# One more mask of every sixteen on GpSimd in a fused pre-norm graph attention block

## The reference

```
h = maximum(layernorm(x), 0)
q, k, v = h @ Wq + bq, h @ Wk + bk, h @ Wv + bv       # split into 16 heads
scores = q @ k.T / sqrt(32);  scores = -inf where adj == 0
out = x + (softmax(scores) @ v) @ Wo + bo
```

## Time and profile before

| what | value |
|---|---|
| median of 3 runs | 1587.12 us (1585.24 to 1588.4) |
| the profiled execution | 1589.11 us, span 1587.3 us |
| mean granted TensorE clock | 0.985 of full speed |
| busy share of PE, DVE, ACT, POOL | 97%, 91%, 89%, 47% |
| masks on GpSimd, on VectorE | 438, 586 |

### The profile page before, as it was taken

One profiled execution on the slowest core, in us unless ns is written; L12 is line 12 of the kernel. 1 busy time (PEld: TensorE's weight loads), 2 busy tenths in 40 slices (PEclk: granted clock), 3 DMA queues, 4 the chain that ended last, 5 costly groups with the idle time before them and its releaser, 6 DMA issues.

```text
span 1587.3 us, 27500 instructions
## 1 busy us (share of the span) xinstructions
PE 1547.2 (97%) x7489; PEld 1040.7 (66%) x7489; DVE 1442.1 (91%) x3505; ACT 1418.9 (89%) x3433; POOL 752.6 (47%) x674
## 2 busy tenths in 40 slices
PE   7899999999999999999999999999999999999987
PEld 6566666666666666666666666676676666666644
DVE  7889899999999989999998999999899999998976
ACT  4899898998989899898998989999899999989884
POOL 3244455454454554455354354454445455353442
PEclk9899999999999999999999999999999999999988
DMA  7544444434444344444434444344444534444320
GB/s 230 124 110 104 129 111 108 137 95 139 101 129 119 101 139 103 130 111 114 132 97 131 101 131 117 93 144 105 125 113 103 143 93 139 101 114 111 99 73 27
DMA packets 154064, 183.63 MB, mean 116 GB/s; under 512 B 67748, under 2 KB 69808, under 8 KB 153904
## 3 DMA queue, kind: packets, MB, share of 16 engines
q1 hardware_dynamic: 149024, 179.76, 42.2%
q10 hardware_dynamic: 4888, 2.11, 0.6%
HBM read 54.79 MB, written 16.78 MB: 45 GB/s over the span
## 4 chain that ended last, share of the span: by engine, by line
PE 56%; DVE 16%; ACT 12%; SPq 7%; issue 7%; DMA 1%; ACTq 1%; DVEq 0%; POOL 0%
PE psP L858 24%; PE psO L950 10%; PE ps L920 10%; PE ps L932 9%; ACT ps L530 6%; DVE ps L688 6%; SPq L283 4%; ACT probs L586 4%; DVE probs L702 3%; SPq L324 2%; DVE neg_max L688 1%; DVE oT_lo L722 1%; ACTq L492 1%; DVE stats L613 1%; DVE probs L705 1%
## 5 line engine op out<-in xcount | busy, mean ns | idle before, releaser
L444 POOL TENSOR_TENSOR probs<-probs,keep_k 128x512 int32<-128x512 int32 x438 | 573.5, 1333 | 559.1 <-ACT probs L586 558.7
L688 DVE CUSTOM_DVE_ANT_0 ps<-ps,bias_q 128x512 f32<-128x512 f32 x1024 | 704.1, 694 | 100.4 <-PE ps L920 94.1
L530 ACT ACTIVATE ps<-ps,neg_max 128x512 f32<-128x512 f32 x1024 | 691.7, 675 | 66.4 <-DVE neg_max L688 49.0
L586 ACT ACTIVATE probs<-ps 128x512 f32<-128x512 f32 x1024 | 622.6, 609 | 52.4 <-PE psO L950 28.0
L920 PE MATMUL ps<-k_stack,q_stack 96*128 96x512 f32 x1024 | 431.5, 422 | 18.7 <-ACT ps L530 13.5
L932 PE MATMUL ps<-q_stack,k_stack 98*128 98x512 f32 x1024 | 421.1, 412 | 5.3 <-ACT probs L586 4.1
L702 DVE SCALAR_TENSOR_TENSOR probs<-turned,probs 128x512 f32<-128x512 bf16 x512 | 371.3, 726 | 5.4 <-ACT probs L586 4.5
L920 PEld LDWEIGHTS ps<-k_stack,q_stack 96*128 96x128 f32 x1024 | 194.8, 190 | 133.6 <-ACT ps L530 53.7
L950 PE MATMUL psO<-probs,v_sb 128*32 128x512 f32 x2048 | 251.7, 609 | 1.2 <-issue 1.2
L932 PEld LDWEIGHTS ps<-q_stack,k_stack 98*128 98x128 f32 x1024 | 196.9, 192 | 72.9 <-ACT probs L586 41.4
L530 ACT ACTIVATION_READ_ACCUMULATOR ps<-ps,neg_max 128x1 f32 x1024 | 223.0, 218 | 0.0
(11 more groups left out here) (87 smaller groups left out, 1891.9 us busy)
## 6 DMA issues: line engine op xcount, KB each, us to landing
k_stack<-oT_hi SPq DMA_DIRECT2D x380, 64.0 KB, 2.0
q_stack<-y_tile SPq DMA_DIRECT2D x360, 64.0 KB, 2.0
x_tile<-in_x_dram SPq DMA_DIRECT2D x66, 256.0 KB, 3.1
y_tile<-in_x_dram SPq DMA_DIRECT2D x62, 256.0 KB, 2.9
out_dram<-y_tile SPq DMA_DIRECT2D x62, 256.0 KB, 2.0
turned<-in_adj_dram SPq DMA_DIRECT2D x61, 256.0 KB, 3.0
q_stack<-part_hi SPq DMA_DIRECT2D x240, 64.0 KB, 2.0
k_stack<-oT_lo SPq DMA_DIRECT2D x196, 64.0 KB, 2.0
```

Source lines behind the costliest of these rows:

```text
L444: nc.gpsimd.tensor_tensor(bits, bits, keep_k[:, kt // 2, :], ALU.mult).then_inc(gpsimd_masked, 1)
L530: nc.scalar.activation(item, item, ACT.Exp, scale=-1.0, bias=neg_max[:, g % 2, col:col + 1], accum_out=exp_sum[:, col:col + 1]).then_inc(e ...
L586: nc.scalar.activation(probs[:, (SLOTS * b + n) % P_RING, :], ps2[:, n % 2, :], ACT.Exp, scale=SCALE).then_inc(exp2_done, 1)
L688: nc.vector.tensor_tensor_reduce(bank1(k, ("s", u)), bank1(k, ("s", u)), bias_q[:, qt, :], -SCALE, 3.0e38, ALU.add, ALU.min, neg_max[:, g ...
```

## The change

Tile 7 of every group joins the list of GpSimd, so that GpSimd masks key tiles 1 and 3 whole (tiles 4 to 7 and 12 to 15) and VectorE key tiles 0 and 2. It holds for all groups but the last two of the last batch. The waits by count follow from the same list.

```
-ON_GPSIMD, LAST_ON_GPSIMD = (4, 5, 6, 12, 13, 14, 15), (4, 12)
+ON_GPSIMD, LAST_ON_GPSIMD = (4, 5, 6, 7, 12, 13, 14, 15), (4, 12)
```

## The result

The kernel with tile 7 on GpSimd has a median of 1588.97 us over 20 runs (1587.03 to 1592.57), beside 1585.33 us (1581.75 to 1588.61) for 20 runs of the kernel before on the same chip. The ratio is 1.0027, with a 95% interval of 1.002 to 1.0035: slower by some 4 us (the medians differ by 3.6 us, and the ratio makes 4.3 us of them), where +3.7 us was forecast.

The account below looks back on a forecast made before the run. TensorE, busy 97% of the span, was taken to bound the kernel, with VectorE second on the chain. Slot delays passing at 16 chain places and in slot 52 summed to +3.7 us on 1587.1, giving 1590.8 us; range 1582 to 1599.

Parts of the forecast that it names:

- slot 4: `form_c` 0.30 us late, passing in 6 steps (1.8 us), less 0.8 us for steps 5 and 13.
- slot 20: `form_c` 0.40 us late, but hidden by VectorE's later waits for TensorE: nothing; 6.0 us with that cover gone.
- slot 36: `form_c` 0.16 us late, passing only in the 8 steps with line 705 on the chain: 1.3 us.
- slot 52: `form_c` 0.52 us late, just fitting under its cover; 0.1 us for each of 14 steps, 1.4 us.
- 8 x 0.16: Slot 36's sum: the 0.16 us delay passes at 8 places where line 705 lies on the chain, 1.3 us.
- the gain of 0.8 us in steps 5 and 13: Slot 4, where `form_c` itself was held before: it would end about 0.8 us earlier, half of it counted each time.
- the third instruction: In slot 4, line 642 of `form_c` is held behind GpSimd's mask of tile 7, ending 0.30 us late.
- signs given for the reader: Line 637's mean about 1 us in slots 20, 36, 52; line 642's maximum above 1; VectorE's busy time falls under 42.
- Hidden delays (1): The delays of `form_c` are hidden and don't reach the end: 1587 to 1589 us; chance 0.28.
- An unheld `form_c` (2): `form_c`'s small instructions get in ahead of the moved mask, so the change is faster: 1580.4 us; chance 0.12.
- All covers gone (3): Every slot of every step passes its delay: 20 us, 1607; more likely half, 1597; chance 0.14.
- The products waiting for GpSimd (4): TensorE's products wait for the moved mask, some 5 us on average, 1592 us; chance 0.04.

Follow-up runs that it names:

- a1: The changed kernel with `form_c` one slot later (slots 5, 21, 37, 53): 1585.77 us, 1.0009 to the kernel before.
- a2: The kernel before with only `form_c` moved one slot later, no mask moved: 1584.87 us, 1.0000.
- e: The kernel before with an unneeded 0.42 us VectorE instruction behind `form_c` in all four slots: 1589.77 us, 1.0030.
- a4: The changed kernel with tile 7 masked by neither engine (GpSimd clears a single column instead): 1583.84 us, 0.9992 to the kernel before.
- b1: The change for tiles 39 and 55 only (slots 36 and 52), against the kernel before: 1588.23 us, 1.0023.
- d52: The kernel before with an unneeded 0.42 us VectorE instruction behind `form_c` in slot 52 alone: 1586.60 us, 1.0007.
- b2: The change for tiles 7 and 23 only (slots 4 and 20), against the kernel before: 1586.18 us, 1.0010.

## Why the prediction was right, and where it wasn't

**The sign and the mechanism held.** The chain of reasons was: the moved mask runs on GpSimd while `form_c` comes up, `form_c` is held to its end, and with TensorE at 97% a late `form_c` costs. Each link has a run: the hold (line 637 at 0.949 us, gone in a1), its price (1.0027 in after, 1.0009 in a1, 1.0000 in a2), lateness alone costing as much (e, with the larger dose), and VectorE's relief being worth nearly nothing (a4). The port rule of the Trainium skill (SBUF — State Buffer, Who interferes with whom) is borne out, by 47 held instructions with two SBUF inputs that end just behind a mask of GpSimd.

**The terms of the sum.** +3.7 us were 1.0 for slot 4, nothing for slot 20, 1.3 for slot 36 and 1.4 for slot 52. That their sum comes so near is in part luck: three of the four delays were put too long and one too short, and the places where they pass were not the ones that the chain had marked.
- Slot 36: the delay was 0.21 us, not 0.16. The step "8 x 0.16", the delay only where line 705 was on the chain, was misplaced: it passes in nearly every step, by way of line 754 to line 883, and of 0.21 us some 0.12 reach TensorE: 1.7 us. In step 5, where the prediction found TensorE's own work on the chain and let nothing pass, line 883 is 0.12 late. A place off the chain was near enough to it.
- Slot 52: the delay was 0.38 us, 0.14 less than forecast, since in nearly every step line 637 gets in first, and with line 640 held in its place less of `form_c` is left behind the end of the mask (0.24 us, not 0.45). Slots 36 and 52 together cost 0.23% in b1, 3.6 us, where 2.7 were forecast. By the traces, TensorE's slot 38 takes 1.5 us more in after than in before, summed over steps 2 to 15, and slots 56 to 60 take 0.6 more. b1 and d52 show that 0.6 as well, but e, which has the same delay in slot 52, shows nothing there, and a2 shows 1.9 at a ratio of 1.0000. So how slot 52 costs isn't settled. The 2.1 us that the trace has for both are inside b1's interval.
- Slots 4 and 20: delays of 0.16 and 0.33 us, forecast 0.30 and 0.40. b2 gives 0.10%, 1.6 us, forecast 1.0; its interval holds nothing too. Of the gain of 0.8 us in steps 5 and 13 little came: `form_c` ended 2.61 us after the start of the read of the row maximum in step 5, against 2.64 before, and 1.96 against 2.29 in step 13. The other six steps of the term (2, 3, 4, 10, 14 and 16) were forecast 0.30 late each; the two traces differ there by between -0.49 and +0.43 us, 0.02 in the mean (step 4 is 0.22 early, 1.98 against 2.20). Both parts of the term were put too large, and they offset each other.

**Which instruction was held.** For slot 4 the price hung on the third instruction, line 642, since it reads two tensors from SBUF. It was held in 2 of 64 cases. Where the first one got in, it was the second, line 640, that was held (26 of 64), and the third then ran free. In slot 4 of step 4 of after:

```profile
359.38 0.52 DVE L637 TENSOR_TENSOR c_all<-neg_max,c_all 128x16 f32<-128x16 f32 x1
359.94 1.22 DVE L640 TENSOR_SCALAR c_parts<-c_all 128x16 fp32r<-128x16 f32 x1
361.19 0.17 DVE L642 SCALAR_TENSOR_TENSOR c_parts<-c_all,c_parts 128x16 fp32r<-128x16 f32 x1
```

The end of `form_c` is set by the end of GpSimd's mask either way: 0.03 us behind it with line 642 held, as the prediction had it for slot 4, 0.24 us with line 640 held, and some 0.45 us with line 637 held alone. Most of the signs given for the reader came true, and three did not: the second hold is line 640's and hardly line 642's; line 637's mean rose to 0.86, 0.98 and 0.85 us in slots 4, 20 and 36, but stayed at 0.19 in slot 52; and VectorE's busy time did not fall by less than 42 us but rose by 10.

**The rivals.** Hidden delays (1) fell with the interval of the result and with e; its 1587 to 1589 us held the measured 1588.97 only because the kernel before ran at 1585.33 beside it, not at the 1587.1 that the figures start from. An unheld `form_c` (2) fell with line 637; its price of -6.7 us was too high as well: a4, with neither mask, gains about 1 us, and 3.6 at the end of its interval. All covers gone (3) would have been 10 to 20 us. The products waiting for GpSimd (4) is not in the trace: what ended TensorE's idle time before line 950, by that line's own view (us, times), was never GpSimd. Nor does the label "issue" hide such a wait: each of the 256 products starts at least 0.55 us after the last GpSimd mask that it needs.

```profile
  issue: 112.9, 350
  ACT probs L586: 10.2, 33
```

## What to carry to other kernels

When work moves from VectorE to GpSimd, ask what VectorE will do while GpSimd does it. If that is an instruction that shares their port, VectorE waits out the slower copy of the very work it was rid of (1.29 us for 0.69), and a tiny instruction pays as much as a large one. Put there an instruction that doesn't share the port or is off the path: moving `form_c` by one slot took back about two thirds of the loss. And when TensorE is at 97%, a delay reaches it in places that one profile's chain does not visit; look at its idle time at the same slot of every step before calling a delay hidden. Taking work away from the late engine need not give the same back: 0.42 us more at four places cost 0.30%, and 0.6 to 0.7 us less at the same places gave 0.08%, with none inside its interval.

## What the hardware showed unexpectedly

- A `tensor_scalar` with a single SBUF input was held as well: line 640, 128x16 from float32 to fp32r, 26 of 64 times, up to 1.22 us in place of 0.175. In a1 the same befell line 631, 128x512 from int32 to bfloat16, at 1.21 in place of 0.42, 14 times. The Trainium skill has it in the same section (SBUF — State Buffer, Who interferes with whom): `tensor_scalar` can enter a mode that uses both port pairs, if its operands meet certain conditions. Before had a `tensor_scalar` that could have warned, line 621: it took up to 1.68 us when it started under a mask of GpSimd, and at most 0.55 otherwise. Line 631 was not held by GpSimd's small line 416 (128x1): of 15 starts under it in after none took over 0.43 us.

```profile
L621 DVE TENSOR_SCALAR x_tile<-x_tile,mean_var,rstd x64: 512/574/1684, 5.6 to 1393.5; 128x512 f32<-128x512 f32 x64
```

- VectorE instructions that read PSUM were not held: lines 688, 754 and 722 keep their length under GpSimd's masks. In before the row maximum of line 688 started 487 times under one, and none took over 0.74 us (median 0.69).
- Held time is counted as busy. VectorE's busy time rose by 10.2 us in after with 62 fewer instructions, and is 39.1 lower in a1 (1413.2) than in after, with the same instructions, for a difference of about 0.2% in time.
